# One transposition for own tiles, a scale row from repeated columns, and a residual added by the transfer to DRAM

## The reference

```python
xn  = layernorm(x, eps=1e-5)
xm  = xn * time_mix + shift(xn) * (1 - time_mix)
k   = exp(min(xm @ Wk.T, 60));  v = xm @ Wv.T;  r = xm @ Wr.T
wkv, sum_k = decaying sums over time of k * v and of k
attn = (sigmoid(r) * wkv / sum_k) @ Wo.T
z   = layernorm(xn, eps=1e-3) * gamma + beta
ffn = clip(z * 128 / max|z|) @ ternary(W) * scale
out = x + attn + ffn
```

## Time and profile before

| what | value |
|---|---|
| median of 3 runs | 892.61 us (891.09 to 892.99) |
| the profiled execution's own time | 891.49 us |
| its span, first to last instruction | 889.7 us |
| TensorE busy | 867.1 us, 97% |
| VectorE busy | 764.8 us, 86% |
| ScalarE busy | 510.3 us, 57% |
| GpSimd busy | 215.2 us, 24% |
| TensorE's granted clock | 1.00 |
| bytes moved by DMA | 107.13 MB |

### The profile page before, as it was taken

One profiled execution on the slowest core, in us unless ns is written; L12 is line 12 of the kernel. 1 busy time (PEld: TensorE's weight loads), 2 busy tenths in 40 slices (PEclk: granted clock), 3 DMA queues, 4 the chain that ended last, 5 costly groups with the idle time before them and its releaser, 6 DMA issues.

```text
span 889.7 us, 12792 instructions
## 1 busy us (share of the span) xinstructions
PE 867.1 (97%) x3984; PEld 714.5 (80%) x3984; DVE 764.8 (86%) x1278; ACT 510.3 (57%) x834; POOL 215.2 (24%) x242
## 2 busy tenths in 40 slices
PE   3989999999999999999999999999999999999998
PEld 2778888888888888888888888888888888888886
DVE  5998999989897999989897897878978888789684
ACT  5584767667594757566564554545546536365441
POOL 5552326242452425240030100200201103011000
PEclk9999999999999999999999999999999999999999
DMA  8222415041423224045643245324451443424311
GB/s 283 108 83 88 149 54 184 13 171 54 165 71 135 101 82 154 12 172 136 212 145 115 84 154 189 125 75 141 153 175 57 157 141 96 154 93 142 95 48 47
DMA packets 59841, 107.13 MB, mean 120 GB/s; under 512 B 7712, under 2 KB 7712, under 8 KB 59808
## 3 DMA queue, kind: packets, MB, share of 16 engines
q1 hardware_dynamic: 59808, 106.73, 35.1%
HBM read 64.76 MB, written 41.96 MB: 120 GB/s over the span
## 4 chain that ended last, share of the span: by engine, by line
PE 90%; DVE 3%; issue 2%; POOL 2%; ACT 1%; DMA 0%; SPq 0%; POOLq 0%; DVEq 0%; ACTq 0%
PE kvr L513 18%; PE kvr L515 18%; PE kvr L514 18%; PE out_banks L552 7%; PE out_banks L554 7%; PE out_banks L534 6%; PE out_banks L533 6%; PE out_banks L531 6%; PE transposed L466 2%; PE out_banks L466 2%; DVE bn_stats L842 1%; POOL normed L1174 1%; POOL own_stats L1156 1%; POOL own_stats L1157 1%; DMA x<-in_x 0%
## 5 line engine op out<-in xcount | busy, mean ns | idle before, releaser
L1247 POOL TENSOR_TENSOR evacuated<-normed,mix_over_ffn_row 128x512 f32<-128x512 f32 x28 | 49.0, 1751 | 339.0 <-DVE ffn_lo L922 339.0
L513 PE MATMUL kvr<-xm_hi,wk_hi 128*128 128x512 f32 x256 | 103.7, 405 | 2.6 <-DVE xm_lo L922 2.6
L513 PE MATMUL kvr<-xm_hi,wv_hi 128*128 128x512 f32 x256 | 102.9, 402 | 2.2 <-DVE wv_lo L927 1.3
L513 PE MATMUL kvr<-xm_hi,wr_hi 128*128 128x512 f32 x256 | 102.7, 401 | 0.0
L515 PE MATMUL kvr<-xm_hi,wk_lo 128*128 128x512 f32 x256 | 101.0, 395 | 0.0
L514 PE MATMUL kvr<-xm_lo,wk_hi 128*128 128x512 f32 x256 | 100.7, 394 | 0.0
L515 PE MATMUL kvr<-xm_hi,wv_lo 128*128 128x512 f32 x256 | 100.2, 391 | 0.0
L515 PE MATMUL kvr<-xm_hi,wr_lo 128*128 128x512 f32 x256 | 100.1, 391 | 0.0
L531 PE MATMUL out_banks<-wo_hi,rwkv_hi 128*128 128x512 f32 x256 | 100.0, 390 | 0.0
L534 PE MATMUL out_banks<-wo_hi,rwkv_lo 128*128 128x512 f32 x256 | 99.7, 389 | 0.0
L514 PE MATMUL kvr<-xm_lo,wr_hi 128*128 128x512 f32 x256 | 99.7, 389 | 0.0
(11 more groups left out here) (140 smaller groups left out, 1922.7 us busy)
## 6 DMA issues: line engine op xcount, KB each, us to landing
other<-ffn_input SPq DMA_DIRECT2D x64, 256.0 KB, 5.1
x<-in_x SPq DMA_DIRECT2D x15, 1024.0 KB, 5.8
other<-in_x SPq DMA_DIRECT2D x8, 1024.0 KB, 5.8
ffn_input<-evacuated SPq DMA_DIRECT2D x32, 256.0 KB, 4.4
ffn_input<-parked SPq DMA_DIRECT2D x32, 256.0 KB, 2.2
attn_scratch<-x SPq DMA_DIRECT2D x8, 1024.0 KB, 4.2
parked<-attn_scratch SPq DMA_DIRECT2D x8, 1024.0 KB, 6.7
out<-parked SPq DMA_DIRECT2D x8, 1024.0 KB, 5.2
```

What stands on the lines that cost most here:

```text
L513: nc.tensor.matmul(KVR[:, m, :], hi, XH[t][:, ch, :], start=(ch == 0), stop=False)
L1247: G.tensor_tensor(U[:, n % RING, :], XN[:, ch, :], BC[:, :], ALU.mult).then_inc(pool_v, 1)
```

## The change

In the first half an own tile is normalised and transposed once, for the attention branch. ScalarE copies each transposed chunk also into a new buffer Y. The feed-forward input is Y times a row: for each token the ratio of the two scales. GpSimd computes the ratio per token (tokens in partitions), TensorE turns it into a row that stands alike in all partitions, by four transposes of a column repeated 128 times (`ratio_row`), ScalarE copies the row to SBUF, and GpSimd multiplies Y by it chunk by chunk (`own_ffn_input`). Slots 0 to 3 and 12 to 15 stay in ScalarE's and VectorE's lists, but TensorE has nothing to do in them ("virtual").

And the attention result of the first half is no longer added by VectorE. SP copies x to the scratch tensor, DRAM to DRAM, at the start of each pass, two transfers of 1 MB. ScalarE copies the four output banks into X (`copy_out`), and GpSimd issues a transfer of X to the scratch tensor that adds to what is there (`add_residual`). SP waits for that transfer before it loads X anew. The first transposes of the run use the output banks instead of the projection banks.

The diff's core:

```diff
+ROW_AFTER = {9: 1, 21: 0}
@@ sync, batch_a
+                for t in range(2):
+                    sp.dma_start(scratch[b, t * TILE:(t + 1) * TILE], x[b, t * TILE:(t + 1) * TILE]
+                                 ).then_inc(s_pre[t], 16)
                 for n in range(7):
                     store_ffn_input(b, n)
...
                 store_ffn_input(b, 12)
-                sp.wait_ge(dve_out, BANKS + bank_use(b, "A", "attn0") + Q)
-                sp.dma_start(scratch_t[b, 0], X[0][:, :, :]).then_inc(s_xst[0], 16)
                 store_ffn_input(b, 13)
-                sp.wait_ge(s_xst[0], 16 * b + 16)
+                sp.wait_ge(s_acc[0], 16 * b + 16)
                 sp.dma_start(X[0][:, :, :], x_t[b + 1, 0]).then_inc(s_x[0], 16)
                 for n in range(14, 19):
                     store_ffn_input(b, n)
...
-                sp.wait_ge(dve_out, BANKS + bank_use(b, "A", "attn1") + Q)
-                sp.dma_start(scratch_t[b, 1], X[1][:, :, :]).then_inc(s_xst[1], 16)
...
-                sp.wait_ge(s_xst[1], 16 * b + 16)
+                sp.wait_ge(s_acc[1], 16 * b + 16)
                 sp.dma_start(X[1][:, :, :], x_t[b + 1, 1]).then_inc(s_x[1], 16)
@@ tensor
+            def ratio_row(k, t, bank):
+                pe.wait_ge(pool_ratio, k + 1)
+                for q in range(Q):
+                    last = nc.tensor.transpose(bank[:, q * P:(q + 1) * P],
+                                               ratio[:, t, q:q + 1].to_broadcast([P, P]), ident[:, :])
+                last.then_inc(pe_row, 1)
+
+            ratio_row(0, 0, TB)
...
                         if j == 0 and ph == "A":
-                            pe.wait_ge(dve_out, first_bank + q + 1)
+                            pe.wait_ge(act_out, first_bank + q + 1)
+                            if q == 0:
+                                pe.wait_ge(act_row, 2 * b + 2 + t)
...
-                    if ph == "B":
+                    if ph == "B" or n is not None and is_virtual(n):
                         n = None
...
+                    if ph == "A" and g in ROW_AFTER:
+                        t = ROW_AFTER[g]
+                        pe.wait_ge(act_out, bank_use(b, ph, f"attn{1 - t}") + 1)
+                        ratio_row(2 * b + 2 - t, t, OUT[:, 0, :])
@@ scalar
+            def copy_row(k, t, bank):
+                act.wait_ge(pe_row, 2 + k + 1)
+                nc.scalar.activation(RROW[:, t, :], bank, ACT.Copy).then_inc(act_row, 1)
...
+                if virtual:
+                    act.wait_ge(pool_z, virtual_before(b, n) + 1)
...
                 elif mix:
                     if ph != "P":
+                        nc.scalar.activation(Y[:, ch, :], bank, ACT.Copy)
...
+            def copy_out(b, t):
+                act.wait_ge(pool_xn, CREDIT + 2 * b + t)
+                act.wait_ge(act_xn, CREDIT + 2 * b + t)
+                for q in range(Q):
+                    act.wait_ge(pe_out, bank_use(b, "A", f"attn{t}") + q + 1)
+                    nc.scalar.activation(X[t][:, q, :], OUT[:, q, :], ACT.Copy).then_inc(act_out, 1)
...
+                    if ph == "A" and g == ATTN0_AFTER + 1:
+                        copy_out(b, 0)
...
                             if ph == "A":
-                                normalise(b, ph, "ffn_own1")
...
+                    copy_out(b, 1)
...
-                elif ph == "A":
-                    normalise(b + 1, ph, "ffn_own0")
@@ vector
-                add_out(b, ph, "attn1")
+                if ph == "B":
+                    add_out(b, ph, "attn1")
@@ gpsimd
             def batch_a(b, is_last=False):
...
-                ffn_scale(*call(b, "own1"), own[:, 1])
-                pool.wait_ge(pe_t, slots_before(b, "A", first_slot("mix_own1") + CH))
-                normalise(XN, X[1], own[:, 1], 1, pool_xn)
+                ffn_scale(*call(b, "own1"), own[:, 1], b, 1)
+                for ch in range(CH):
+                    own_ffn_input(b, first_slot("ffn_own1") + ch)
                 other(b, "other1")
+                add_residual(b, 0)
                 mix_scale(*mix_call(b, "A", "next0"), own[:, 0])
...
+                ffn_scale(*call(b, "next0"), own[:, 0], b + 1, 0)
                 if not is_last:
+                    for ch in range(CH):
+                        own_ffn_input(b + 1, first_slot("ffn_own0") + ch)
+                add_residual(b, 1)
+                if not is_last:
                     other(b + 1, "other0")
+
+            def add_residual(b, t):
+                pool.wait_ge(s_pre[t], 16 * b + 16)
+                pool.wait_ge(act_out, BANKS + bank_use(b, "A", f"attn{t}") + Q)
+                G.dma_start(scratch_t[b, t], X[t][:, :, :], accum_op=ALU.add).then_inc(s_acc[t], 16)
+
+            def own_ffn_input(b, n):
+                kind, ch = SLOTS[n]
+                t = int(kind[-1])
+                pool.wait_ge(act_row, 2 * b + t + 1)
...
+                G.tensor_tensor(Y[:, ch, :], Y[:, ch, :], RROW[:, t, :], ALU.mult).then_inc(pool_z, 1)
```

More of the change, by code:

```diff
@@ L149, in mixed_decay_kernel @@
         s_xst = [sem(f"x_stored{t}") for t in range(2)]
+        s_acc = [sem(f"residual_added{t}") for t in range(2)]
+        s_pre = [sem(f"residual_laid_out{t}") for t in range(2)]
         s_oth = sem("other_loaded")
@@ L221, in slots_before, with is_virtual, pe_slots_before, virtual_before @@
             return n if ph == "P" else CH + len(SLOTS) * b + n
+        def is_virtual(n):
+            return SLOTS[n][0].startswith("ffn_own")
+        def pe_slots_before(b, ph, n):
+            if ph == "P":
+                return n
+            per_batch = sum(not is_virtual(k) for k in range(len(SLOTS)))
+            return CH + per_batch * b + sum(not is_virtual(k) for k in range(n))
+        def virtual_before(b, n):
+            return 2 * CH * b + sum(is_virtual(k) for k in range(n))
         def ffn_stores_before(b, n):
@@ L251, in normed_count @@
             if ph == "A":
-                return 4 * b + [k for k in SLOT_KINDS if "other" not in k].index(kind) + 1
-            return 4 * HALF + 2 * (b - HALF) + ["mix_own1", "mix_next0"].index(kind) + 1
+                return 2 * b + ["mix_own1", "mix_next0"].index(kind) + 1
+            return 2 * HALF
         def stats_number(b, ph, tile):
@@ L288, in shifted @@
             return E[:, n % 2, :] if ph == "P" and n > 1 else WS[:, n % 2, :]
-        first_banks = [TB[:, :]] + [KVR[:, i, :] for i in range(3)]
+        first_banks = [OUT[:, q, :] for q in range(Q)]
         def slot_bank(ph, n):
@@ L672, in normalise @@
                 ffn = kind.startswith("ffn")
-                i = 4 * b if kind == "ffn_own0" else stats_number(b, ph, tile)
-                act.wait_ge(pool_step, STEPS + steps_before(i, ph) + (OTHER_STEPS if "other" in kind else STEPS if ffn else MIX_STEPS))
+                i = stats_number(b, ph, tile)
+                act.wait_ge(pool_step, STEPS + steps_before(i, ph) + (OTHER_STEPS if "other" in kind else MIX_STEPS))
                 for q in ACT_CHUNKS:
@@ L707, in _ @@
                 high_part(0, "P", m)
[L708 to L712, removed]
             weight_hi("r")
+            for ch in range(CH):
+                last = nc.scalar.activation(Y[:, ch, :], first_banks[ch], ACT.Copy)
+            last.then_inc(act_first, 1)
+            copy_row(0, 0, TB[:, :])
             act.wait_ge(dve_w, 3 * CH)
@@ L757, in batch @@
                     part1_first = ahead_of_part2(n)
+                    if ph == "A" and g - 1 in ROW_AFTER:
+                        t = ROW_AFTER[g - 1]
+                        copy_row(2 * b + 2 - t, t, OUT[:, 0, :])
                     if part1_first:
@@ L1181, in _ @@
             normalise(XN, X[0], own[:, 0], 0, pool_xn)
[L1182 to L1184 removed]
+            ffn_scale(0, 0, own[:, 0], 0, 0)
             pool.wait_ge(s_w[1], 16)
@@ L1232, in batch_a @@
                 if not is_last:
-                    ffn_scale(*call(b, "next0"), own[:, 0])
-                    pool.wait_ge(pe_t, slots_before(b, "A", len(SLOTS)))
-                    normalise(XN, X[0], own[:, 0], 1, pool_xn)
+                    for ch in range(CH):
+                        own_ffn_input(b + 1, first_slot("ffn_own0") + ch)
+                add_residual(b, 1)
+                if not is_last:
                     other(b + 1, "other0")
+            def add_residual(b, t):
+                pool.wait_ge(s_pre[t], 16 * b + 16)
+                pool.wait_ge(act_out, BANKS + bank_use(b, "A", f"attn{t}") + Q)
+                G.dma_start(scratch_t[b, t], X[t][:, :, :], accum_op=ALU.add).then_inc(s_acc[t], 16)
@@ L1252, in batch_b @@
                         mix_input(b, n)
+            for ch in range(CH):
+                own_ffn_input(0, first_slot("ffn_own0") + ch)
             other(0, "other0")
```

75 lines of the change are left out of this document (47 added, 28 removed).

## The result

The changed kernel takes **1009.25 us** (median of 4 runs, 1007.84 to 1011.28) where the kernel before took 892.43 beside it: a ratio of 1.131, 95% interval 1.129 to 1.134. The forecast was 961 with a range of 918 to 992: the sign was right, the size was not. The profiled execution took 1009.55 us, its span 1007.8, which is 118.1 us longer than before.

What follows compares the result with a forecast made beforehand. TensorE, busy 98.76 of 98.86 us a pass, was taken as the bound. X[0] reload 30.0, X[1] reload 27.6, row groups 1.8, ScalarE 2.0 and stalls 7.0 summed to 68.4 us more, giving 961; range 918 to 992.

Steps and rivals of the forecast that it cites:

- The products ... so 0: GpSimd's 32 new products: 30 us more work in four passes, needed only behind an 11 us output projection, priced at 0.
- The reload of X[0]: End of first output projection to slot 20: X[0] returns late behind GpSimd's adding transfer, 7.5 us four times, 30.0 in all.
- A: Time from GpSimd's issue of an adding transfer to its landing, taken as load plus store, 7.9 us.
- After a stall: TensorE's work after a long idle is dearer: 1.0 us for each of seven stalls, 7.0 in all.
- The reload of X[1]: Pass start to slot 8: store 0 queues behind the add, X[1]'s load and two copies, 9.2 us three times, 27.6.
- P: Time of one 1 MB DRAM-to-DRAM copy on SP's queue, ahead of store 0, taken as 3.8 us.
- The transition: End of the first half into the second, whose code only counts its waits from other numbers: 0 us.
- ScalarE, 0 to 3.0 a pass: Slots 8 to 11: four more copies and a row on ScalarE; 0.5 us a pass taken, 2.0 in all.
- The rival at 882.5: X[0] and store 0 arrive in time and only TensorE's list, 10.1 us shorter, counts: 882.5 us; chance 5%.
- The rival with the add as cheap as a store: The adding transfer lands in 4.2 us like a plain store: run of 935 us; chance 20%.
- the dear add (12): Rival: writing out and adding is dearer than its bytes, 12 us to landing: run of 990 us; chance 15%.
- the copies do hold store 0: Forecast's queue on SP before slot 8; the rival that they do not hold it gave 926 us, chance 25%.

Runs made afterwards that it cites:

- the eased kernel: Changed kernel with its DRAM copies later, an extra early reduction, and each pass's first adding transfer issued before GpSimd's last four steps on the other tile: 961.71 us.
- the early one: Changed kernel with one more partition_all_reduce, of a constant, on GpSimd ahead of the last adding transfer: 1002.05 us.

## Why the prediction was wrong, step by step

- **"The products ... so 0"** (GpSimd) is the step that failed worst. They were hidden from their reader, as said, but not from VectorE, which was not asked. They cost 26 us when taken out alone (4.3 in the opening, the rest in slot 8 to T0 and slot 20 to T1), in a sum that had nothing for it. The rows to ask stood there: VectorE was busy 25.37 of 27.09 and 22.97 of 23.67 us in just these stretches. An engine with 90.35 of 98.86 is not "not the bound": of 2.6 us more in it, 2.1 reached TensorE, and the lower clock behind that wait came on top.
- **The reload of X[0], "A - 0.4"**: right mechanism, three sizes off. A is 9.6 for 7.9, 7 us in four passes (the sum for it, 5.8 + 4.2 - 2.2, is 7.8 by itself). GpSimd's issue, "T0 + 6.4", came at T0 + 9.4 to 9.8 in three passes, 10 us; it was read in one pass, and two of the four passes before already had the last step end at T0 + 7.7 and 7.8. The load of X[0] took 6.3 for 5.8, 2 us. With these, 30.0 becomes 48.7, and T0 to slot 20 measured 48.6. That it is the issue is shown by the eased kernel.
- **After a stall, 1.0, seven times**: nothing of the 7.0 shows in the two stretches it was meant for. TensorE's work there is 1.6 and 2.4 us longer by the granted clock, but slots 8 and 20 start when GpSimd has normalised X all the same, and both stretches add up without the term. The clock counts elsewhere: behind the short waits for VectorE, which the forecast did not have (0.95 in slot 8 to T0). Read from rows; no run changed the clock alone.
- **The reload of X[1], "A + 2P - 6.3"**: the mechanism is shown. That 27.5 us were measured for 27.6 is luck: P was over by 1.2, twice, A under by 1.5 and the transfer's start by 0.8.
- **The transition, priced at 0 with the second half**: wrong. GpSimd's first reduction stood behind a transfer that came late, and lost the idle time that had covered its preparation. With the early one the last T1 to the end is 9.5 of the 11.3 us shorter; the whole run gained 7.2, as its first half took 2.1 longer.
- **ScalarE, 0 to 3.0 a pass**: without the products slot 8 to T0 is 0.4 to 0.5 us longer than before, so its copies cost no more than the 0.5 taken; no run took them out. **TensorE's list**: 1.9 us less in a pass, but only 1.8 us of the run, because X[0] comes no earlier. The rival at 882.5 is out even for the transposition alone.
- The rival with the add as cheap as a store would have been right about a plain store (4.7 for 4.2), the dear add (12) was too dear, and the copies do hold store 0.
- The range: its upper end took in each case at its likeliest price, but no term for an engine's work becoming slower beside another's. That the sum at all the high ends, 1010, is the time measured is luck too: it was made of other terms.

## What to carry to other kernels

Ask of each instruction that goes to an idle engine not only who waits for it, but which engine beside it slows down; in a stretch where the second engine is over nine tenths busy, nothing that holds it is free. A short wait of TensorE can cost more than itself, where, as here, its granted clock falls behind it. What a transfer does for an engine is paid in its latency, where a buffer's reload stands behind it: here 20 us of VectorE's adds were exchanged for 88 us. And a first call of a rare instruction belongs where its engine idles.

## What the runs showed that I had not expected

A 1 MB transfer that adds takes 9.6 us to land, 4.9 more than the same transfer without the addition. GpSimd's two-operand product of 128x512 (1.72 us) lengthens VectorE's pair of scans from 2.86 to 4.57 us; a one-operand one (0.97 us) to 3.21. The first partition_all_reduce needs 5.7 to 8.8 us ahead of it, once. Behind waits of 8.54 and 11.41 us TensorE came back at a granted clock of 0.50, the lower of its two levels; behind one of 2.14 us the clock over the stretch was 0.94.
